# A one-core perceiver block with state-space scan and routed experts: groups of 2,4,4,4,2 batches instead of four of 4, an earlier first expert wave, and the key bias moved into the exponential

## The chip, the cores and the metric

One Trainium2 chip, one of its cores. The metric is the device time of one execution in microseconds, the median of several runs. All arithmetic is 32-bit floating point.

## What is computed

Sixteen batches of 64 tokens, width 512, go through three blocks with residual connections; each batch has a context of 512 rows.

```python
x = x + xattn(layernorm(x), ctx, ctx)        # softmax(q k^T / 8) v with biases bq, bk, bv
x = x + mamba(layernorm(x))                  # 1024 channels, 16 states per channel:
    xc    = silu(conv4(x @ Wx))
    delta = softplus(x @ Wdt + b)
    h     = exp(delta * A) * h + delta * B_t * xc       # for each token in turn
    y     = sum_s h_s * C_ts + D * xc ;   out = y @ Wout
x = x + ffn(layernorm(x))                    # 16 experts, 4 for each token, chosen by a
                                             # grouped top-k on sigmoid(x @ Wg) + e_bias
```

The reference reshapes queries and keys so that each batch falls into two independent attention units (even and odd rows of tokens and context): 8 heads x 32 queries = 256 query rows against 256 keys. There are 32 units. The key bias gives a term q·bk that is the same for all keys of a query row.

## The kernel before

**Groups.** The batches are worked off in groups (`GBS`, L58): four groups of 4 batches, that is 256 tokens, 2 token tiles of 128 and 8 attention units each. A group goes through attention and the projections (B and C, delta, x with its convolution). Its 16 states are then scanned while the *next* group is in attention. One state (`scan_step`, L1308) is four VectorE passes over 128 x 2048: input product L1317, scan L1320, product with C (L1324 or L1327), and, where it is done on VectorE, the addition to y (L1331). ScalarE makes the decay of each state before (`scan_decay`, L1072, eight exponentials).

**Sums on TensorE.** For groups 0 to 2 (`SUMMED`, L105) the addition to y is done by TensorE instead: `start_sum` (L655) and `sum_state` (L661) multiply by the identity into four PSUM banks, 8 instructions of 512 columns for a state, and `copy_sum` (L1055) takes the sum out. For group 3 VectorE adds (L1331).

**An attention unit.** `scores` (L669): 16 matmul instructions of 256 columns (L677), and for each half of the query rows one more with 8 rows of contraction that adds the key-bias term to every key (L678, 4 instructions for a unit). VectorE takes the negated maximum (`neg_max`, L1256), ScalarE exponentiates with that as bias (L969) and normalises, TensorE transposes the probabilities (L687) and multiplies by the context (L699, 16 instructions). Before the units of a group stands `attn_prep` (L606): queries L613, key-bias term L619, queries times key weights L643; behind them the value projection L730, then `projections` (L744, L759), and at the end of the loop `out_proj` (L767) for the group before.

**Scan beside attention.** In each stage four states run in the preparation (`LEAD`), eight beside the units (`unit_states`, L110), two before and two behind the layer norm of the next group (`TAIL`, `PRE`). The end of a stage on VectorE is `scan_inputs` (L1289, its second pass is L1295), after which the next group's scan can start.

**Experts.** Tokens are routed (`ffn_norm`, `ffn_logits`, `route`, `positions`, `slots`) and scattered by GpSimd into DRAM rows grouped by expert (`dispatch`, L1605), which must have been cleared to zero first (L1598 to L1603, 40 transfers of up to 1 MB from a zero tile, gated on score units 8 to 15). `WAVES` (L68) splits the groups in two waves: groups 0 to 2, 6 tiles, 39 blocks of 128 rows; group 3, 2 tiles, 23 blocks. A block is: transposes L788, gate and up L798 (8 instructions of 512 columns), hidden on ScalarE and VectorE (L1138, L1468, L1469), transposes L807, down L819 (4 instructions), and 2 MB of DMA, three quarters of it expert weights. The loop `experts` (L823) runs the same order on PE, ACT and DVE; wave 0 begins only when group 2 has been routed, which happens after the attention of group 3, and SyncE's queue waits there for the block table (`expert_of`, L417) and for all tokens dispatched (L447). Beside wave 0, `scan_parts` (L116) lays out the 14 states of group 3 that are left, spread over steps -1 to 28. `OUT_STEP` (29 = 39 - `REST`) is the step behind which the output projection and the routing of group 3 stand in every engine's order. Two PSUM banks each serve for the transposed blocks (0, 1) and for the block outputs (4, 5). Wave 1 follows; GpSimd gathers each token's four expert rows (`collect`, L1614), VectorE combines them (L1477), SyncE stores the tile.

The order on every engine is written out by hand in these loops; PE, ACT, DVE, POOL and the SP queue each follow their own in-order program and wait on semaphores.

Of the kernel before, what the change touches and what calls it, by code (L numbers as in the profile page):

```python
# [27 lines left out]
P = 128  # L28
# [29 lines left out]
GBS = (4, 4, 4, 4)  # L58
# [9 lines left out]
WAVES = ((0, 1, 2), (3,))  # L68
# [7 lines left out]
CLEARS = [(w, r, min(r + CLEAR_ROWS, ROWS[w])) for w in range(len(WAVES)) for r in range(0, ROWS[w], CLEAR_ROWS)]  # L76
CLEAR_UNITS = range(8, 16)
# [3 lines left out]
REST = 10  # L81
OUT_STEP = BLOCKS[0] - REST
# [19 lines left out]
LEAD, TAIL, PRE = 4, 2, 2  # L102
LN_AFTER = 3
SCAN_PARTS = 4
SUMMED = range(NGR - 1)  # L105
# [4 lines left out]
def unit_states(g, k):  # L110

    n = NS - LEAD - TAIL - 2
    return list(range(LEAD + k * n // NUS[g + 1], LEAD + (k + 1) * n // NUS[g + 1]))


def scan_parts(q):  # L116

    n0 = 2 * SCAN_PARTS
    return [(n // SCAN_PARTS, n % SCAN_PARTS) for n in range(n0, NS * SCAN_PARTS)
            if (n - n0) * (BLOCKS[0] + 1 - REST) // (NS * SCAN_PARTS - n0) - 1 == q]  # L120


def a_jobs():

    out = [("norm", 0)] * NTS[0]
    for g in range(NGR):
# [3 lines left out]
        out += [("query_ctx", g)] * (DC * DC // 2)  # L130
# [21 lines left out]
def perceiver_block(nc, x, ctx_t, ctx_n, wq_t, wk_w, wv_t, xp_t, dt_t, bc_t, ow_t, gate_t,  # L152
                    eg_t, eu_t, ed_t, params, bc_dram, out):
    with ExitStack() as es:
# [52 lines left out]
        rsum = sb("row_sum", 2 * QB)  # L207
        ones8 = sb("ones", 1)
# [32 lines left out]
        wb_ = [sb(f"expert_w_{s}", 2 * DC * I + IC * D)[:, :] for s in range(NW)]  # L241
        w_gu = [v[:, 0:2 * DC * I].rearrange("p (g c i) -> p g c i", g=2, c=DC) for v in wb_]
        w_dn = [v[:, 2 * DC * I:].rearrange("p (c d) -> p c d", c=IC) for v in wb_]
        xbT = [sb(f"block_x_t_{s}", D)[:, :].rearrange("p (c t) -> p c t", c=DC) for s in range(2)]
        route_ = sb("route_scratch", 4 * QB * KEYS)
# [4 lines left out]
        xb = [sb(f"block_x_{s}", D)[:, :] for s in range(NX)]  # L250
        yb = [sb(f"block_y_{s}", D)[:, :] for s in range(NX)]
        pick_ = sb("route_pick", TOPK * 6 * E)
        sb("unused_2", 2 * SW - NX * 2 * D - TOPK * 6 * E)
        acc_last = sb("y_acc", SW)
        acc_s = [(dA[(NS * (g + 1) - 1) % NDEC] if g in SUMMED else acc_last)[:, 0:NBK * GTS[g]] for g in range(NGR)]
        acc = [v.rearrange("p (k t) -> p k t", k=NBK) for v in acc_s]

        def route_buffers(c):

            n = NT * E * E  # L260
            if c < NGR - 2:
                return hs_[:, 0:n], hs_[:, n:2 * n], hs_[:, 2 * n:2 * n + 2 * TOPK * NT * E]
            return route_[:, 0:n], route_[:, n:2 * n], pick_[:, :]
# [53 lines left out]
        sb8_rdy = sem("qbk_ready")  # L317
        q_full = sem("ctx_queries_full")
# [19 lines left out]
        cleared = sem("dispatch_rows_cleared")  # L338
# [23 lines left out]
        D_LAST = sum(NTS) + sum(NTS[:NGR - 1])  # L362
# [14 lines left out]
        def _(sp):  # L377
# [104 lines left out]
            for g in range(NGR - 1):  # L482
# [9 lines left out]
                for s in range(NS - TAIL, NS):  # L492
                    load_bc(g * NS + s)
                load_proj(g + 1)
                store_bc(g + 1)
                load_bc((g + 1) * NS)
                load_bc((g + 1) * NS + 1)
            sp.wait_ge(ys_rdy, NGR)
            load_bc((NGR - 1) * NS + 2)
            for w in range(len(WAVES)):  # L500
                n = BLOCKS[w]
                if w == 0:
                    for j in range(NW):
                        load_gate_up(w, j)
                        load_down(w, j)
                    for j in range(NX):
                        load_block_x(w, j)
                    load_bc((NGR - 1) * NS + 3)
                for j in range(-2, n + 1):
# [15 lines left out]
                    if w == 0:  # L525
                        for state, part in scan_parts(j - 1):
                            if part == SCAN_PARTS - 1 and state + 2 < NS:
                                load_bc((NGR - 1) * NS + state + 2)
# [9 lines left out]
        def _(pe):  # L538
# [67 lines left out]
            def attn_prep(g):  # L606
# [15 lines left out]
                if g > 0:  # L622
                    start_sum(g - 1)
# [8 lines left out]
                for c in range(DC):  # L632
                    for mp in range(2):
# [13 lines left out]
                        if mp == 0:  # L647
                            mm.then_inc(q_full, 1)
# [1032 lines left out]
```

## Time and profile before

| | us |
|---|---|
| median of 3 runs (1382.69 to 1383.88) | 1383.72 |
| the profiled execution | 1382.23 |
| its span, first to last instruction | 1380.4 |
| TensorE busy with matmuls | 1190.3 (86%) |
| VectorE busy | 871.5 (63%) |
| ScalarE busy | 629.5 (46%) |
| DMA moved | 266 MB, mean 193 GB/s |

The profiled execution lies 1.5 us under the median, and 1.8 us of it lie outside the span. Busy shares are averages over stages with different limits. The busy time of matmuls is modelled and overlaps, so the pace of a loop is better read from the distance between two starts of the same step than from busy time. A row of the chain of waits gives start, length and what ran; the next start minus the last is the pace.

### The profile page before, as it was taken

The numbers are of one execution on the slowest core, as the hardware profiler recorded it, in microseconds if no ns is written. First come the engines' busy times: TensorE is split into PE (matmuls) and PEld (weight loads), VectorE is DVE, ScalarE is ACT, GpSimd is POOL, SyncE is SP. The second block draws the span as 40 slices with busy tenths as digits, with TensorE's granted clock in tenths as the row PEclk, the third lists the DMA queues.
The fourth block names the chain that finished last, engine by engine and source line by source line (L and its number), as shares of the span: only waits on it lengthen the run. The fifth ranks groups of instructions, "written<-read, shape, count | busy, mean of one in ns | idle before, by whom it ended". The sixth has DMA issues, their size and how long they took to land.

```text
span 1380.4 us, 13494 instructions
## 1 busy us (share of the span) xinstructions
PE 1190.3 (86%) x4404; PEld 738.6 (54%) x4404; DVE 871.5 (63%) x882; ACT 629.5 (46%) x1394; POOL 132.5 (10%) x113
## 2 busy tenths in 40 slices
PE   5996869888897899999799999835999999999993
PEld 4774745555574566666456666532444444544451
DVE  1211279655858779785897987685999993323312
ACT  4442566334356745536665563642545441222231
POOL 0010002211000006000003300011000000223002
PEclk9998989889999999999999999957999998999997
DMA  7346104999510034440013424018899993999993
GB/s 271 101 136 256 42 16 141 407 406 328 181 61 8 16 91 154 129 143 12 16 36 99 148 61 141 5 49 295 318 374 359 367 373 115 370 364 407 411 387 122
DMA packets 114038, 266.22 MB, mean 193 GB/s; under 512 B 10161, under 2 KB 43057, under 8 KB 113969
## 3 DMA queue, kind: packets, MB, share of 16 engines
q1 hardware_dynamic: 98096, 207.16, 43.3%
q0 software_dynamic: 15872, 58.20, 10.8%
q8 instruction: 36, 0.59, 0.2%
q14 instruction: 34, 0.27, 0.1%
HBM read 197.03 MB, written 68.29 MB: 192 GB/s over the span
## 4 chain that ended last, share of the span: by engine, by line
PE 60%; DVE 22%; ACT 7%; DMA 7%; issue 3%; POOL 1%; SPq 0%; POOLq 0%; DVEq 0%; ACTq 0%
PE bank L665 10%; PE bank L677 9%; PE bank L798 8%; PE bank L699 7%; PE bank L759 7%; DVE state L1320 6%; PE bank L819 4%; DVE state L1317 3%; PE bank L678 3%; DMA ctx<-in_ctx_t 3%; DVE state L1327 2%; DVE y_acc L1331 2%; PE bank L613 2%; PE bank L730 2%; ACT decay L1082 2%
## 5 line engine op out<-in xcount | busy, mean ns | idle before, releaser
L1320 DVE TENSOR_TENSOR_SCAN state<-decay,state 128x2048 f32<-128x2048 f32 x64 | 282.9, 4420 | 22.0 <-ACT decay L1082 21.1
L798 PE MATMUL bank<-expert_w,block_x_t 128*128 128x512 f32 x496 | 226.3, 599 | 3.0 <-ACT block_x_t L1134 2.6
L665 PE MATMUL bank<-decay,params 128*128 128x512 f32 x384 | 178.7, 610 | 5.1 <-DVE decay L1324 5.1
L1082 ACT ACTIVATE decay<-delta_even,params 128x256 f32<-128x256 f32 x256 | 107.2, 499 | 115.2 <-PE bank L665 106.7
L1611 POOL DMA_INDIRECT dispatched<-ffn_x,slot x32 | 71.0, 2218 | 796.3 <-DVE slot L1413 787.7
L677 PE MATMUL bank<-ctx,queries_ctx 128*128 128x256 f32 x512 | 133.2, 406 | 13.8 <-DMA ctx<-in_ctx_t 12.6
L798 PEld LDWEIGHTS bank<-expert_w,block_x_t 128*128 128x128 f32 x496 | 91.2, 194 | 94.6 <-issue 91.5
L1082 ACT ACTIVATE decay<-delta_odd,params 128x256 f32<-128x256 f32 x256 | 106.3, 499 | 56.8 <-PE bank L665 47.1
L699 PE MATMUL bank<-probs,ctx 128*128 128x256 f32 x512 | 121.8, 393 | 11.2 <-ACT probs L991 6.8
L699 PEld LDWEIGHTS bank<-probs,ctx 128*128 128x128 f32 x512 | 99.8, 197 | 37.6 <-issue 16.7
L819 PE MATMUL bank<-expert_w,hidden_t 128*128 128x512 f32 x248 | 117.0, 594 | 2.9 <-ACT hidden_t L1148 2.9
L677 PEld LDWEIGHTS bank<-ctx,queries_ctx 128*128 128x128 f32 x512 | 97.5, 200 | 40.6 <-issue 15.7
L665 PEld LDWEIGHTS bank<-decay,params 128*128 128x128 f32 x384 | 71.2, 193 | 88.0 <-issue 81.3
L759 PE MATMUL bank<-normed_t,queries_ctx 128*128 128x256 f32 x512 | 113.6, 382 | 4.3 <-DMA queries_ctx<-in_dt_t 3.2
L1468 DVE SCALAR_TENSOR_TENSOR hidden<-hidden,bank 128x256 f32<-128x256 f32 x62 | 26.1, 421 | 143.0 <-ACT hidden L1138 136.0
L1324 DVE TENSOR_TENSOR decay<-state,bc_bcast 128x2048 f32<-128x2048 f32 x48 | 109.5, 2282 | 0.8
L759 PEld LDWEIGHTS bank<-normed_t,queries_ctx 128*128 128x128 f32 x512 | 97.4, 191 | 22.6 <-issue 4.5
L1317 DVE TENSOR_TENSOR state<-u_even,bc_bcast 128x2048 f32<-128x2048 f32 x32 | 73.4, 2293 | 36.6 <-DMA bc_bcast<-bc_scratch 35.7
L1138 ACT ACTIVATE hidden<-bank 128x256 f32<-128x256 f32 x62 | 23.6, 381 | 145.7 <-PE bank L798 136.7
L819 PEld LDWEIGHTS bank<-expert_w,hidden_t 128*128 128x128 f32 x248 | 46.8, 190 | 61.1 <-issue 57.4
L1317 DVE TENSOR_TENSOR state<-u_odd,bc_bcast 128x2048 f32<-128x2048 f32 x32 | 73.3, 2290 | 2.0 <-DMA bc_bcast<-bc_scratch 1.3
L1144 ACT ACTIVATE block_y<-bank 128x512 f32<-128x512 f32 x62 | 37.0, 597 | 80.7 <-PE bank L819 76.7
(193 smaller groups left out, 1391.8 us busy)
## 6 DMA issues: line engine op xcount, KB each, us to landing
dispatched<-ffn_x POOLq DMA_DIRECT2D x38, 1024.0 KB, 22.8
expert_w<-in_eg_t SPq DMA_DIRECT2D x62, 512.0 KB
expert_w<-in_eu_t SPq DMA_DIRECT2D x62, 512.0 KB
expert_w<-in_ed_t SPq DMA_DIRECT2D x62, 512.0 KB
ctx<-in_ctx_t SPq DMA_DIRECT2D x32, 512.0 KB, 6.9
ctx<-in_ctx_n SPq DMA_DIRECT2D x32, 512.0 KB, 4.2
bc_bcast<-bc_scratch SPq DMA_DIRECT2D x64, 256.0 KB, 5.9
block_x<-dispatched SPq DMA_DIRECT2D x62, 256.0 KB
```

The costliest lines, as they stand in the source:

```text
L665: mm = pe.matmul(y_bank[c][:, :], ident, dA[(g * NS + j) % NDEC][:, c * 512:(c + 1) * 512], start=False, stop=(j == NS - 1))
L677: pe.matmul(o, QT[g][:, k, c, qb * P:(qb + 1) * P], ctxT[n % 2][:, c, :], start=(c == 0), stop=False)
L678: mm = pe.matmul(o, sb8[g][:, k, qb * 4:(qb + 1) * 4, :], ones8[0:H, :].to_broadcast([H, KEYS]), start=False, stop=True)
L699: mm = pe.matmul(b[:, cc * Q:(cc + 1) * Q], ctxN[n % 2][:, j, c * P:(c + 1) * P], probT[n % 2][:, j, :], start=(j == 0), stop=(j == KC - 1))
L759: mm = pe.matmul(b[:, kk * gt:(kk + 1) * gt], w[:, c, (k + kk) * P:(k + kk + 1) * P], xT[g][:, c, :], start=(c == 0), stop=(c == DC - 1))
L798: mm = pe.matmul(o, xbT[q % 2][:, c, :], w_gu[q % NW][:, :, c, :], start=(c == 0), stop=(c == DC - 1))
L819: mm = pe.matmul(bank[4 + q % 2][:, :], hidT[q % 2][:, c, :], w_dn[q % NW][:, c, :], start=(c == 0), stop=(c == IC - 1))
L1082: ins = act.activation(dA[n % NDEC][:, k * gt:(k + 1) * gt], dlt[g][:, k, :], ACT.Exp, scale=par[:, c:c + 1])
L1317: step(dve.tensor_tensor(h3, u[g], bs, ALU.mult))
L1320: dve.tensor_tensor_scan(h, dA[n % NDEC][:, 0:sw], h, 0.0, ALU.mult, ALU.add).then_inc(scan_rd, 1)
L1324: dve.tensor_tensor(hc, h3, cs, ALU.mult).then_inc(step_done, 1)
L1611: pool.indirect_dma_start(xd[WAVE_OF[c]], bass.IndirectOffsetOnAxis(slot[:, i:i + 1].bitcast(U32), 0), fx[:, t, :], None).then_inc(dispatc ...
```

## The change

- Groups of 2, 4, 4, 4, 2 batches: 5 groups, the first and last with 128 tokens, one tile, 4 units and states 1024 wide. `GBS = (2, 4, 4, 4, 2)`.
- Waves (0,1,2) and (3,4): 5 tiles and 35 blocks, then 3 tiles and 27 blocks. Group 2 is routed during the attention of group 4, so nothing of wave 0's routing stands behind the last projections.
- Sums on TensorE for groups 1 and 2, and for the first 11 states of group 3; the rest (group 0, the last 5 states of group 3, group 4) is added on VectorE.
- The last 5 states of group 3 and all 16 of group 4 run beside the first steps of wave 0, laid out by weight (a scan counts double, a group by its batches). Output projection and routing of group 3 come at step 10, 11 and 13, those of group 4 at 28, 29 and 31 (`REST` 7).
- The key-bias matmuls L678 go; `row_bias` makes the term as one column for each unit half in `attn_prep`, ScalarE copies it, and `neg_max` takes it off and puts it on again in two small VectorE passes.
- One PSUM bank for block transposes (0) and one for block outputs (1), since banks 4 and 5 serve the output projections in wave 0.
- The clearing of wave 0's rows (24 transfers) moves to units 1 to 11, that of wave 1 (16 transfers) to units 14 to 21, and takes its zeros from cleared rows in DRAM.
- Weights of blocks 0 and 1 and the first three x blocks are fetched before the last group's y is started; the weights of block 2 behind it.

```diff
-GBS = (4, 4, 4, 4)
+GBS = (2, 4, 4, 4, 2)
-WAVES = ((0, 1, 2), (3,))
+WAVES = ((0, 1, 2), (3, 4))
-CLEAR_UNITS = range(8, 16)
+CLEAR_UNITS = [range(1, UNIT0[2]), range(UNIT0[2] + 2, UNIT0[3] + 2)]
-REST = 10
-OUT_STEP = BLOCKS[0] - REST
+REST = 7
-LEAD, TAIL, PRE = 4, 2, 2
+LEAD = 4
+UNIT_STATES = [NS - 8] * (NGR - 2) + [4]
+TAIL = [2] * (NGR - 2) + [1]
+PRE = [2] * (NGR - 2) + [2]
-SUMMED = range(NGR - 1)
+SUM_END = {g: NS for g in range(1, NGR - 2)}
+SUM_END[NGR - 2] = LATE
+def scan_work():
+    n0, n1 = (NGR - 2) * NS + LATE, NGR * NS
+    todo = [(n, p, GBS[n // NS] * (2 if p == 1 else 1)) for n in range(n0, n1) for p in range(SCAN_PARTS)]
+    total = sum(v for _, _, v in todo)
+    out = {j: [] for j in range(-1, BLOCKS[0])}
+    gone = 0
+    for n, p, v in todo:
+        out[gone * (BLOCKS[0] + 1 - REST) // total - 1].append((n, p))
+        gone += v
+    return out
+OUT_STEP = {NGR - 2: step_of((NGR - 1) * NS - 1, SCAN_PARTS - 1) + 1, NGR - 1: BLOCKS[0] - REST}
...
+            def row_bias(g):
                 pe.wait_ge(sb8_rdy, g + 1)
+                b = job_a()
+                for k in range(NUS[g]):
+                    for qb in range(QB):
+                        mm = pe.matmul(b[:, k * QB + qb:k * QB + qb + 1], sb8[g][:, k, qb * 4:(qb + 1) * 4, :], ones8[0:H, :],
+                                       start=True, stop=True)
+                mm.then_inc(a_full, 1)
...
-                        pe.matmul(o, QT[g][:, k, c, qb * P:(qb + 1) * P], ctxT[n % 2][:, c, :], start=(c == 0), stop=False)
-                    mm = pe.matmul(o, sb8[g][:, k, qb * 4:(qb + 1) * 4, :], ones8[0:H, :].to_broadcast([H, KEYS]),
-                                   start=False, stop=True)
+                        mm = pe.matmul(o, QT[g][:, k, c, qb * P:(qb + 1) * P], ctxT[n % 2][:, c, :],
+                                       start=(c == 0), stop=(c == DC - 1))
...
+                step(dve.tensor_reduce(nm, bank[n % 2][:, :].rearrange("p (b k) -> p b k", b=QB), AX_X, ALU.max, negate=True))
+                if k == 0:
+                    dve.wait_ge(rowb_rdy, g + 1)
+                step(dve.tensor_tensor(nm, nm, add, ALU.subtract))
+                dve.tensor_tensor(nm, nm, add, ALU.add).then_inc(nm_rdy, 1)
...
-                if q >= 2:
-                    pe.wait_ge(xt_rdy, q - 1)
+                if q >= 1:
+                    pe.wait_ge(xt_rdy, q)
...
+                    for c, out_step in OUT_STEP.items():
+                        if w == 0 and j == out_step:
+                            out_proj(c)
+                        if w == 0 and j == out_step + 1:
+                            ffn_logits(c)
+                        if w == 0 and j == out_step + 3:
+                            positions(c)
```

## Rows read from the trace of the kernel before

**Rows 1.** The chain of waits, whole span: start us, us, what (ends of stages).
```profile
174.94 2.30 DVE queries_ctx L1295
...
422.57 2.30 DVE queries_ctx L1295
...
656.66 2.30 DVE queries_ctx L1295
...
886.94 2.30 DVE queries_ctx L1295
...
950.22 4.20 PE bank L798 x8
```
**Rows 2.** The same chain: units of the first stage and of the third.
```profile
79.57 3.65 PE bank L699 x16
88.56 3.65 PE bank L699 x16
...
542.91 3.63 PE bank L665 x8
546.54 3.45 PE bank L699 x16
555.34 3.63 PE bank L665 x8
```
**Rows 3.** Table by stretch: busy PE, PEld, DVE, ACT, POOL, PEclk, DMA share, GB/s.
```profile
245.00:350.00 105.00, 85.93 (x302) 57.30 (x301) 57.37 (x31) 45.22 (x115) 18.35 (x25) 0.89 0.98 381
...
736.00:820.00 84.00, 81.68 (x325) 56.27 (x325) 68.37 (x46) 46.05 (x117) 25.28 (x8) 1.00 0.33 110
...
880.00:950.00 70.00, 27.97 (x97) 19.49 (x96) 50.84 (x96) 26.66 (x55) 13.31 (x8) 0.62 0.32 113
950.00:1138.00 188.00, 180.76 (x546) 90.39 (x544) 180.15 (x116) 91.54 (x218) 0.00 (x0) 1.00 0.96 348
```
**Rows 4.** The chain of waits in the expert waves.
```profile
1062.90 4.43 DVE state L1320
...
1075.91 4.44 DVE state L1320
...
1217.89 3.70 PE bank L798 x8
...
1346.94 3.44 PE bank L798 x8
```
**Rows 5.** Groups of instructions, the key-bias matmul: xcount, busy us, mean ns, idle before.
```profile
L678 PE MATMUL bank<-ones,normed 8*128 8x256 f32 x128 | 45.2, 432 | 0.0
```
**Rows 6.** Timeline, PE and DVE: the first score, and small operations used as prices.
```profile
36.86 1.97 PE L677 MATMUL bank<-ctx,queries_ctx 128*128 128x256 f32 x8 [1.19 <-issue]
...
688.87 1.93 PE L581 MATMUL bank<-gate_weights,probs 128*128 128x16 f32 x16 [0.87 <-ACTq L898]
...
696.10 0.69 DVE L1349 TENSOR_TENSOR state<-state,params 128x512 f32<-128x512 f32 x1
```
**Rows 7.** DMA issues, us 245 to 350: xcount, KB each, us to landing.
```profile
ctx<-in_ctx_t SPq DMA_DIRECT2D x6, 512.0 KB, 18.2
```
**Rows 8.** Timeline behind step 29: output projection and routing of group 3.
```profile
1138.71 15.67 PE L777 MATMUL bank<-out_w,y_acc 128*128 128x512 f32 x32 [1.74 <-issue]
...
1154.42 0.69 DVE L1266 TENSOR_TENSOR x_tokens<-x_tokens,bank 128x512 f32<-128x512 f32 x1 [6.18 <-PE bank L777]
...
1157.41 1.00 DVE L1251 TENSOR_SCALAR ffn_x<-x_tokens,mean_var,rstd 128x512 f32<-128x512 f32 x2
...
1165.61 0.18 DVE L1361 TENSOR_SCALAR route_score<-route_logits 128x32 f32<-128x32 f32 x1 [5.28 <-ACTq L904]
...
1173.98 0.19 DVE L1390 TENSOR_TENSOR route_score<-route_score,route_group 128x32 f32<-128x32 f32 x1
```
**Rows 9.** Timeline of the tail: the combination of the last two tiles.
```profile
1368.79 3.11 DVE L1477 SCALAR_TENSOR_TENSOR x_tokens<-y_top,top_weight,x_tokens 128x512 f32<-128x512 f32 x4 [17.08 <-DMA y_top<-expert_out,expert_out_slot]
...
1374.87 3.12 DVE L1477 SCALAR_TENSOR_TENSOR x_tokens<-y_top,top_weight,x_tokens 128x512 f32<-128x512 f32 x4 [2.97 <-DMA y_top<-expert_out,expert_out_slot]
```

More of the change, by code:

```diff
@@ L110, in unit_states, with summed, sum_count, step_of @@
 def unit_states(g, k):
-    n = NS - LEAD - TAIL - 2
+    n = UNIT_STATES[g]
     return list(range(LEAD + k * n // NUS[g + 1], LEAD + (k + 1) * n // NUS[g + 1]))
[L116 to L120, printed above, removed]
+def summed(n):
+    return n // NS in SUM_END and n % NS < SUM_END[n // NS]
+def sum_count(n):
+    return sum(summed(k) for k in range(n + 1))
+def scan_work():
[8 more added lines that the diff above has]
+    return out
+SCAN_WORK = scan_work()
+def step_of(n, part):
+    return next(j for j, v in SCAN_WORK.items() if (n, part) in v)
+OUT_STEP = {NGR - 2: step_of((NGR - 1) * NS - 1, SCAN_PARTS - 1) + 1, NGR - 1: BLOCKS[0] - REST}
 def a_jobs():
@@ L207, in perceiver_block @@
         rsum = sb("row_sum", 2 * QB)
+        rowb_ = sb("row_bias", 2 * NU * QB)
+        rowb = [rowb_[:, g % 2 * NU * QB:(g % 2 + 1) * NU * QB] for g in range(NGR)]
         ones8 = sb("ones", 1)
@@ L337, in perceiver_block @@
         zero_rdy = sem("zero_rows_ready")
-        cleared = sem("dispatch_rows_cleared")
+        cleared = [sem(f"dispatch_rows_cleared_{w}") for w in range(len(WAVES))]
         cst_rdy = sem("index_constants_ready")
@@ L525, in _ @@
                     if w == 0:
-                        for state, part in scan_parts(j - 1):
-                            if part == SCAN_PARTS - 1 and state + 2 < NS:
-                                load_bc((NGR - 1) * NS + state + 2)
+                        for k, part in SCAN_WORK.get(j - 1, []):
+                            if part == SCAN_PARTS - 1 and k + 2 < NGR * NS:
+                                load_bc(k + 2)
                     elif j % 2 == 0 and (j - 6) // 2 in range(len(WTILES[0])):
@@ L740, in attention @@
                 if g > 0:
-                    for s in range(NS - TAIL - PRE, NS - PRE):
+                    for s in range(TAIL0[g - 1], PRE0[g - 1]):
                         sum_state(g - 1, s)
@@ L1109, in projections @@
             def projections(g):
-                late = list(range(NS - TAIL + 1, NS)) if g > 0 else []
+                late = list(range(TAIL0[g - 1] + 3, min(NS, LATE + 2 if g == NGR - 1 else NS))) if g > 0 else []
                 norm_std(NTS[g])
@@ L1116, in projections @@
                     proj_dt(g, k)
-                    if late:
+                    if late and k in (0, NBK - 2):
                         scan_decay(g - 1, late.pop(0))
@@ L1536, in _ @@
                             out_slots(0)
-                late = list(range(NS - TAIL - 2, NS))
-                for s in range(TAIL):
-                    scan_step(g, late.pop(0))
+                for s in range(TAIL0[g], PRE0[g]):
+                    scan_step(g, s)
                 add_tiles(g + 1)
@@ L1545, in _ @@
                     norm_apply(TILE0[g + 2], NTS[g + 2], NT, mv1_, rstd1, TILE0[g + 2])
-                for s in range(PRE):
-                    scan_step(g, late.pop(0))
+                for s in range(PRE0[g], PRE0[g] + PRE[g]):
+                    scan_step(g, s)
                 for k in range(0, NBK, 2):
@@ L1622, in collect @@
                         .then_inc(yg_in[n % 2], 16)
-            for c in range(NGR):
+            pool.wait_ge(zero_rdy, 1)
+            clear(0)
+            dispatch(0)
+            clear(1)
+            for c in range(1, NGR):
                 dispatch(c)
```

237 lines of the change are left out of this document (124 added, 113 removed).

## The prediction

> **What bounds the kernel now.** I read the chain of waits first, to cut the span into stages at VectorE's `scan_inputs` (L1295): the stages end at 174.9, 422.6, 656.7 and 886.9 us, so they last 174.9, 247.6, 234.1 and 230.3 us, and then 63.3 us pass until the first gate matmul of the experts [rows 1]. Inside a stage the chain shows TensorE: a unit of the first stage takes 8.99 us, one of a later stage 12.43 us, of which 3.44 us more are the sum of one state [rows 2]. The table by stretch confirms it, TensorE 81.7 of 84 us busy, VectorE only 68.4 [rows 3]. Two stretches stand out. Between 880 and 950 TensorE is busy 28 of 70 us at a mean clock of 0.62: group 2 is routed, dispatched and its blocks fetched, with nothing else to do. Between 245 and 350 the DMA engines are 0.98 busy and TensorE loses 19 us: the clears. In wave 0 the chain goes over to VectorE: two blocks and one state of group 3 come every 13.01 us, against a block every 5.87 us in wave 1 (22 distances from 1217.89 to 1346.94), where TensorE and nearly the DMA set the pace [rows 4].
>
> **The change, stage by stage.** The sum is made against the profiled execution (span 1380.4, time 1382.23); the median of the runs is 1.5 us higher.
>
> *Key bias.* An L678 instruction has 256 columns like those of L699, 16 of which take 3.45 us in the chain, so 0.216 us each (0.217 with the seams); 4 in a unit are 0.87 us and 128 are 27.8 us (the 45.2 us of its group are overlapping busy time) [rows 2, 5]. The new `row_bias` has 128 instructions of one column. The nearest row has 16 columns and the same 128 weights to load: 16 in 1.93 us, 0.12 us each, so 15 us [rows 6]. It stands where ScalarE's copies and VectorE's states set the pace, so I put 0.5 us on the path in each stage; the ends are 0 and 3 us for each. The Trainium skill (TensorE: Matmul & The Clock Gate, Wait — 56ns, not 53.3ns?) has the gap between matmuls as the number of columns in cycles, by which `row_bias` would be nearly free; the row of L581 speaks against it, and the sum with the rule would be some 2 us shorter. The two small VectorE passes are about 0.2 us each. They lie in a unit where VectorE has 10.5 of 11.6 us to do, and in the first stage where it idles.
>
> *Narrow states.* No row has 1024 columns. A pass of 512 takes 0.69 us and one of 2048 2.30 us [rows 1, 6], 1.04 ns a column, so 1024 take 1.22 us (between 1.15, half of 2.30, and 1.3); a scan 4.43/2 + 0.03 = 2.25 us [rows 4]. A narrow state, added on VectorE, is 3 x 1.22 + 2.25 + gaps = 6.0 us; a wide one 11.35 us.
>
> *Stage 0* (2 batches, 4 units). The first score stood at 36.9 us [rows 6]; with half the width before it, but fixed costs kept, 28.5. 8 units at 8.99 were 72 us; 4 at 8.99 - 0.87 = 8.13 are 32.5. The other 66 us (ends of the unit pipeline, value, norm, projections, convolution) become 48, half wide where columns count, bound in part by ScalarE's fixed costs, and with the statistics of the other tiles now in the last unit, 3 us of them. 109 us, **-66**.
>
> *Stage 1* (8 units beside group 0). I start from stage 3, which had no contention, 230.3 us. Units at 8.13 instead of 12.43 take off 34; eight sums outside the units and `start_sum`, 9 x 3.6 us, take off 31, some of it through decays that are half as wide: 165. Then the clears: 24 of 1 MB in 11 units of stages 0 and 1 instead of 38 in 8. Per unit there are 2.2 MB of clears, 1.05 of context, 0.2 of B and C, 3.4 MB in 8.1 us, 420 GB/s: over the 381 GB/s of the saturated stretch [rows 3], at which a unit takes 9.0 us. I charge 8 us, all of it here (0 to 32, below): 173 us, **-75**.
>
> *Stages 2 and 3* are as before less 8 x 0.87 us and plus 0.5 us of `row_bias`; stage 2 has the 16 clears from DRAM to DRAM beside it, for which no row exists: 3 us (0 to 10). 231 and 224 us, **-3 and -6**.
>
> *Stage 4* is new (4 units, 11 wide states of group 3). From the 224 us of stage 3: 4 units of 11.56 less, 46; the projections' 128 matmul instructions at 0.12 instead of 0.217 us, 12; value 4; one tail state less before the norm, partly hidden, 4. `block_table` and `out_slots` now stand in unit 1 on a nearly full VectorE, 5 more. The 4 MB of projection weights that are fetched a fifth time land behind the norm and wait for nothing new; if they do, up to 5 us. **+162**. Stages together: 899 us for 886.9, +12.
>
> *The gap* between the last `scan_inputs` and the first gate matmul was 63.3 us [rows 1]. Tokens are dispatched and weights fetched a stage earlier; what is left is the rest of `scan_inputs`, y's start (8 narrow copies) and a copy of the block: 6 us, **-57**. What it hid (group 2's output projection) is in stage 4.
>
> *Wave 0* lasted from 950.2 to 1217.9, 267.7 us [rows 1, 4]. After: 5 wide states, 56.8 us, 16 narrow ones, 96 us, and 29 hidden pairs of 0.86 us, 25 us, are 178 us in 29 slots, 6.1 a block; TensorE needs 5.87. New are group 3's output projection and routing in the middle of it. VectorE idled some 14 us while the 15.67 us of L777 ran, then took 4 us to the end of the norm and 8.6 us for `route`, and slots and waits are 4 more [rows 8]. That was harmless behind the last state; now VectorE bounds on both sides, so 31 us count. With 4.5 us before the first hidden and 3 of friction: 216.5 us. From there to wave 1: 7.8 us for one tile of L777, then 5 gate and 7 down matmul groups with their transposes, 37 us, logits and positions 4: 49 us of TensorE. The data chain beside it is a little longer: 11 us from the projection's end to the logits as in [rows 8], 7 `route`, 8 to the positions (they wait for step 31), 2 slots, 6 dispatch, 6 landing, 3 for the block: 52 us. Together 268 us, **0**, though there are 4 blocks fewer.
>
> *Wave 1* has 27 blocks for 23: 4 x 5.87 = **+23.5**. A single bank for transposes and one for outputs I put at nothing: ScalarE, busy 92 of 188 us even in wave 0 [rows 3], copies them within the step, before the next use a step later; if decays hold it up, a copy's 0.6 us for each such block. *The tail* has a third tile, and two tiles are 6.1 us apart: **+6** [rows 9].
>
> Sum: -66 - 75 - 3 - 6 + 162 - 57 + 0 + 23.5 + 6 = -15.5 us. Span 1365, execution 1367, median 1368 us.
>
> **Rivals.**
>
> *Clears stop the first stages* (slower). While the clears had the queues, a context load took 18.2 us to land [rows 7]. Loads are issued two units ahead of their scores, so at that latency a unit can't be shorter than about (18.2 + 4)/2 = 11 us, 3 over 8.1, and 11 units lose 32 us instead of my 8: 1392 us. It decides if clears queue up, that is if more than about 8.1 x 0.4 = 3.2 MB fall in a unit; the sum above has 3.4, just over. For it: the saturated stretch. Against it: there 5 MB of clears fell in a unit of 12.4 us, and a backlog of 23 built up that can't build up with two or three in a unit. 0.12. The Trainium skill (DMA: Bandwidth & Descriptors, Queues, rings and completion order) has each engine take its queues in turn, by which a context load would wait for few clear packets, and this rival would fall; the 18.2 us of [rows 7] don't bear out an even share.
>
> *Waves don't mesh* (about no change). The routing of group 4 now has 7 steps instead of 10 to reach the dispatched rows, SyncE's queue stops at step 31 for the block table with the store of block 30 and the down weights of block 33 behind it, and wave 0's states slip past their slots. If the middle stall is 40 and the seam 8 us more, +17: 1385 us. 0.13.
>
> *The early stages give more* (faster). No contention (-8), narrow stages' fixed costs smaller (-8), and part of the stall around step 10 filled, because TensorE can run a block ahead (-8): 1344 us. For it: ScalarE is only 46% busy. 0.23.
>
> *It doesn't do what it says*: wave 0 is held at its start by the dispatch or by weights and the gap stays half, +25, 1393. Group 2's slots come in unit 1 of stage 4, over 80 us before; 0.03.
>
> **The numbers.** The forecast, 1368 (its own reach 1355 to 1380), has 0.49. A measurement of this kernel can tell about 0.2%, 2.8 us, from no change. Faster: the forecast, the fast rival and a little of the second, 0.76. Same: 0.08. Slower: the first and fourth rival and the rest, 0.16. The range goes from the fast rival with some room, 1338, to the contention rival, 1392.
>
> **What would show it.** The stages' ends at about 109, 282, 513, 737 and 899 us; units of 8.1 to 9 us in the first two stages and 11.6 after; the first L798 near 905; in wave 0 VectorE idle for some 14 us before L1266 at step 10; wave 1 from about 1173. If the ends of stages 0 and 1 come 20 us late with waits for `ctx`, the first rival holds; if the first L798 lies above 930, the gap did not close.

## The result, and the profile after

The changed kernel takes 1436.34 us (median of 4 runs, 1433.52 to 1441.55) against 1383.2 for the kernel before (4 runs): a ratio of 1.0397, 95% interval 1.0365 to 1.0429. Forecast were 1368 us and a range of 1338 to 1392. It is 53 us slower where 15 us less were expected. The profiled execution took 1441.55 us, its span is 1439.8.

The first view is the timeline of VectorE in the changed kernel, the second pass of `scan_inputs` (now L1361), whose five starts end the stages; the summary gives the shortest, median and longest duration in ns and the first and last start of each group.

```profile
L1361 DVE SCALAR_TENSOR_TENSOR queries_ctx<-queries_ctx,u_even x3: 1224/1227/2293, 114.7 to 955.7; 128x1024 f32<-128x1024 f32 x2, 128x2048 f32<-128x2048 f32 x1
L1361 DVE SCALAR_TENSOR_TENSOR queries_ctx<-queries_ctx,u_odd x2: 2291/2292/2292, 303.7 to 783.7; 128x2048 f32<-128x2048 f32 x2
```

The third of the `u_even` starts is at 555.57. With the first gate matmuls of wave 0 (962.66) and wave 1 (1249.92), from the chain of waits, the span falls into the pieces of the forecast. The last column is experiment e4, told below.

| piece | forecast | after | e4, clears moved |
|---|---|---|---|
| stage 0 | 109 | 114.7 | 107.6 |
| stage 1 | 173 | 189.0 | 168.8 |
| stage 2 | 231 | 251.9 | 225.5 |
| stage 3 | 224 | 228.1 | 227.2 |
| stage 4 | 162 | 172.0 | 170.6 |
| gap to wave 0 | 6 | 7.0 | 7.0 |
| wave 0 | 268 | 287.3 | 284.1 |
| wave 1 and tail | 192 | 189.9 | 189.2 |
| span | 1365 | 1439.8 | 1379.9 |

Three pieces stand out, stages 1 and 2 and wave 0. The chain of waits of the changed kernel shows what stands there (start us, us, what). It answers to [rows 2] and [rows 4]:

```profile
168.64 14.98 DMA ctx<-in_ctx_t
183.67 5.52 PE bank L732 x16
194.38 10.11 DMA ctx<-in_ctx_t
204.53 5.33 PE bank L732 x16
215.04 9.55 DMA ctx<-in_ctx_t
...
405.64 3.46 PE bank L732 x16
412.53 3.47 PE bank L753 x16
416.01 0.37 SPq L428
416.44 0.46 SPq L452
416.94 34.24 DMA ctx<-in_ctx_t
451.23 6.55 PE bank L732 x16
...
1092.98 13.41 DMA bc_bcast<-bc_scratch
...
1144.48 11.07 DMA bc_bcast<-bc_scratch
...
1176.31 8.81 DMA bc_bcast<-bc_scratch
```

In the units of [rows 2] the chain was TensorE from end to end. Now three context loads of 9.6 to 15 us stand in stage 1, one of 34 us in stage 2, and loads of B and C in wave 0. Those of stage 1 are not new: the chain of the kernel before has two there too, in the stretch with its clears, which [rows 2] does not cover:

```profile
253.13 17.65 DMA ctx<-in_ctx_t
...
288.70 17.69 DMA ctx<-in_ctx_t
```

New are the load in stage 2, which had no clears before, and the B and C loads of wave 0, of which the kernel before has none in its chain. The list of waits of the changed kernel says the same in sums (us in total, times, longest):

```profile
DVE state L1383 <- DMA bc_bcast<-bc_scratch: 66.1, 16, 23.9
...
PE bank L732 <- DMA ctx<-in_ctx_t: 44.1, 6, 24.0
...
ACT row_bias L1006 <- PE bank L704: 25.2, 5, 6.7
```

The timeline of stage 2, DMA issues and scores, shows who is ahead of the late load:

```profile
406.16 1.54 SPq L420 DMA_DIRECT2D ctx<-in_ctx_t  x1
406.77 2.02 POOL L1677 DMA_INDIRECT dispatched<-ffn_x,slot  x1 [0.30 <-issue]
408.78 3.96 POOL L1668 DMA_DIRECT2D dispatched<-dispatched  x8
...
416.94 0.46 SPq L420 DMA_DIRECT2D ctx<-in_ctx_t  x1
...
420.17 0.96 POOL L1668 DMA_DIRECT2D dispatched<-dispatched  x2 [7.43 <-PE bank L732]
...
427.21 15.43 SPq L452 DMA_DIRECT2D bc_bcast<-bc_scratch  x1
442.68 4.01 SPq L420 DMA_DIRECT2D ctx<-in_ctx_t  x1
449.82 2.29 DVE L1383 TENSOR_TENSOR state<-u_odd,bc_bcast 128x2048 f32<-128x2048 f32 x1 [23.86 <-DMA bc_bcast<-bc_scratch]
...
451.23 6.55 PE L732 MATMUL bank<-ctx,queries_ctx 128*128 128x256 f32 x16 [24.03 <-DMA ctx<-in_ctx_t]
```

Read it from the second row down. GpSimd finishes the dispatch of group 0 (L1677), for whose slots it had waited since its last clear in stage 1, and then issues **eight** clears of 1 MB within 4 us. Their gates are 14 to 17 score units, two for each, but in its in-order program they stand behind the dispatch, and by then all four gates had passed. The context load issued at 416.94 lands 34 us later, the next B/C issue takes 15.43 us on SyncE's queue, and TensorE and VectorE both stand still for 24 us. An average over the stage hides this. The table by stretch, for stage 2 after and then in e4 (columns as in [rows 3], with instruction counts), has the same work in both and even the lower DMA share where the wait is. A stretch of 10 us inside the wait, the third fence, shows what the average hides: the DMA engines are 0.98 busy, at 334 GB/s, and nothing else runs.

```profile
303.70:555.60 251.90, 203.37 (x820) 141.49 (x819) 184.24 (x168) 128.31 (x286) 18.38 (x18) 0.89 0.41 130
```
```profile
276.30:501.90 225.60, 200.12 (x816) 139.11 (x815) 184.24 (x168) 128.49 (x286) 17.34 (x16) 0.94 0.46 135
```
```profile
430.00:440.00 10.00, 0.00 (x0) 0.00 (x0) 0.00 (x0) 0.00 (x0) 0.00 (x0) 0.50 0.98 334
```

With the two clears of 420.17, ten of 1 MB were issued in 12 us. At 334 GB/s they and the loads beside them take some 31 us or more (an estimate from these rows), about the 34 us that the context load took.

### The profile page after: what moved, and what is told of

Its sections match the earlier page's. It is cut to its first block, busy times and chain, and to the rows that moved or that the text cites. A ratio compares the mean times of both kernels' runs of the same rounds, so it can differ in the third digit from the quotient of the medians.

```text
span 1439.8 us, 14536 instructions
## 1 busy us (share of the span) xinstructions
PE 1186.8 (82%) x4662; PEld 774.0 (54%) x4662; DVE 913.8 (63%) x1084; ACT 675.7 (47%) x1602; POOL 122.7 (9%) x113
## 3 DMA queue, kind: packets, MB, share of 16 engines
q0 software_dynamic: 12096, 58.20, 10.8%
## 4 chain that ended last, share of the span: by engine, by line
PE 53%; DVE 21%; DMA 11%; ACT 10%; issue 3%; SPq 2%; POOL 1%; POOLq 0%; DVEq 0%; ACTq 0%
PE bank L720 8%; PE bank L852 8%; PE bank L813 7%; DVE state L1386 6%; PE bank L732 6%; DMA ctx<-in_ctx_t 6%; PE bank L753 5%; PE bank L871 4%; ACT decay L1145 3%; DVE state L1383 3%; DMA bc_bcast<-bc_scratch 2%; PE bank L784 2%; PE bank L655 2%; PE bank L704 2%; PE bank L685 2%
## 5 line engine op out<-in xcount | busy, mean ns | idle before, releaser
L1386 DVE TENSOR_TENSOR_SCAN state<-decay,state 128x2048 f32<-128x2048 f32 (+1 forms) x80 | 285.5, 3568 | 39.6 <-ACT decay L1145 38.4
L852 PE MATMUL bank<-expert_w,block_x_t 128*128 128x512 f32 x496 | 234.3, 617 | 1.0 <-ACT block_x_t L1199 1.0
L732 PE MATMUL bank<-ctx,queries_ctx 128*128 128x256 f32 x512 | 130.6, 415 | 48.1 <-DMA ctx<-in_ctx_t 44.1
L720 PE MATMUL bank<-decay,params 128*128 128x512 f32 x344 | 162.5, 618 | 0.0
L1145 ACT ACTIVATE decay<-delta_even,params 128x128 f32<-128x128 f32 (+1 forms) x384 | 132.4, 427 | 40.2 <-PE bank L720 33.7
L732 PEld LDWEIGHTS bank<-ctx,queries_ctx 128*128 128x128 f32 x512 | 105.4, 210 | 68.3 <-DMA ctx<-in_ctx_t 45.9
L1677 POOL DMA_INDIRECT dispatched<-ffn_x,slot x32 | 65.6, 2050 | 728.1 <-DVE slot L1481 719.9
L813 PE MATMUL bank<-normed_t,queries_ctx 128*128 128x256 f32 (+1 forms) x640 | 120.2, 351 | 8.8 <-DMA queries_ctx<-in_dt_t 5.4
L813 PEld LDWEIGHTS bank<-normed_t,queries_ctx 128*128 128x128 f32 x640 | 107.3, 202 | 24.5 <-DMA queries_ctx<-in_dt_t 6.5
L1383 DVE TENSOR_TENSOR state<-u_even,bc_bcast 128x1024 f32<-128x1024 f32 (+1 forms) x48 | 75.9, 1581 | 40.7 <-DMA bc_bcast<-bc_scratch 39.6
L1390 DVE TENSOR_TENSOR decay<-state,bc_bcast 128x2048 f32<-128x2048 f32 x43 | 98.1, 2282 | 0.8
```

The costliest lines, as they stand in the source:

```text
L720: mm = pe.matmul(y_bank[c][:, :], ident, dA[(g * NS + j) % NDEC][:, c * 512:(c + 1) * 512], start=False, stop=(j == SUM_END[g] - 1))
L732: mm = pe.matmul(o, QT[g][:, k, c, qb * P:(qb + 1) * P], ctxT[n % 2][:, c, :], start=(c == 0), stop=(c == DC - 1))
L813: mm = pe.matmul(b[:, kk * gt:(kk + 1) * gt], w[:, c, (k + kk) * P:(k + kk + 1) * P], xT[g][:, c, :], start=(c == 0), stop=(c == DC - 1))
L852: mm = pe.matmul(o, xbT[q % 2][:, c, :], w_gu[q % NW][:, :, c, :], start=(c == 0), stop=(c == DC - 1))
L1145: ins = act.activation(dA[n % NDEC][:, k * gt:(k + 1) * gt], dlt[g][:, k, :], ACT.Exp, scale=par[:, c:c + 1])
L1383: step(dve.tensor_tensor(h3, u[g], bs, ALU.mult))
```

## The experiments

Each ratio is to the kernel before on the same chip, with its 95% interval. Lengths of stages come from the starts of `scan_inputs` in each trace, as above.

**e1: the key bias alone.** The kernel before, with `row_bias`, its copy and the two small passes instead of L678, that is, from L678 to the last line on `neg_max` in the diff above.

> The kernel before with the key bias in the exponential and nothing else of the change. Theory A (the size is what the units show): a unit of the changed kernel's second stage is 10.8 us long where one of before is 12.4, so the four key-bias matmuls cost 1.65 us and not 0.87; 32 units give 53 us back, row_bias makes ScalarE wait 5.3 us in each of 4 preparations, 21 us: net 25 to 32 us faster, 1352 to 1358. Rival B (my forecast's sizes, 0.87 us a unit and 0.5 us a stage): 26 us faster in stages, 2 to 7 us for each stage of 8 units, with units of 11.6 us. Rival C: VectorE's two small passes and row_bias eat it up, within 5 us of before. The length of a unit in the third stage tells A (10.2 to 10.8) from B (11.6); the preparation's length tells the cost of row_bias.

1377.37 us, ratio 0.9951 (0.9932 to 0.997). The unit of stage 2 went from 12.43 to 10.78 us: an L678 costs 0.41 us, not 0.217. The 432 ns "mean of one" in [rows 5], which I had put aside as overlap, was nearly right. But the preparation, from the end of a stage to the first score, grew from 58.5 us (422.57 to 481.02) to 68.3 (425.02 to 493.32). Its timeline:

```profile
470.12 6.63 PE L665 MATMUL bank<-ones,normed 8*128 8x1 f32 x32 [3.48 <-ACT queries_ctx L955]
...
476.79 0.18 ACT L963 ACTIVATE row_bias<-bank 128x16 f32<-128x16 f32 x1 [6.33 <-PE bank L665]
...
482.40 3.30 ACT L1100 ACTIVATE decay<-delta_odd,params 128x256 f32<-128x256 f32 x8 [5.43 <-PE bank L679]
```

ScalarE's copy of 16 columns lies between the copies of queries and the next decay, and ScalarE stands still for 6.33 us until the 32 instructions of one column are through. Most of what the units of a stage gain, 8 x 1.65 = 13.2 us, is given back there. Theory A had the unit right and the total wrong: 6 us faster, not 25 to 32, nearest to rival C.

**e2: B/C loads of wave 0 on GpSimd's queue.**

```diff
-sp.dma_start(bcs[k % 2] ...)      # in SyncE's program, beside wave 0
+pool.dma_start(bcs[k % 2] ...)    # in GpSimd's, behind the dispatch
```

> The changed kernel, with the loads of B and C beside wave 0 issued from GpSimd's queue, which idles there, instead of behind the expert weights on SyncE's queue. Theory A (a queue's order): in wave 0 VectorE waits 13.4, 11.1 and 8.8 us for bc_bcast because their issue stands behind the wait of SyncE's queue for a block; the waits go, and wave 0 (287 us from its first gate matmul to wave 1's) gets 20 to 30 us shorter, 1406 to 1416. Rival B (DMA traffic, or VectorE's own work, sets wave 0): the waits stay or move into the passes, less than 8 us.

1445.01 us, ratio 1.0451, and 288.7 us between the first gate matmuls of the waves, for 287.3: nothing gained. The chain shows each load still as a piece of its own:

```profile
1121.34 8.02 DMA bc_bcast<-bc_scratch
...
1136.61 8.52 DMA bc_bcast<-bc_scratch
...
1152.31 7.79 DMA bc_bcast<-bc_scratch
...
1167.35 7.86 DMA bc_bcast<-bc_scratch
```

SyncE's queue was not the cause. As rival B said, the waits stay. A load starts when the state two before it is done and lands 8 us later; a narrow state takes 6.

**e3: wave 1's clears late; e4: all clears in the preparations.** The clears are gated on scan states of the preparation instead of score units: in e3 wave 1's in the preparation of stage 3; in e4 also wave 0's, half in that of stage 1 from the zero tile, half in that of stage 2 from cleared rows in DRAM.

```diff
-pool.wait_ge(s_full, CLEAR_UNITS[w][...])
+pool.wait_ge(step_done, g * NS + s)      # s = 1, 2, 3; dl_rdy for the first quarter
```

> The changed kernel, with the 16 DRAM-to-DRAM clears of wave 1's rows moved from the units of stage 2 to the preparation of stage 3's successor stage, where the DMA engines idle. Theory A (clears hold up context loads): the wait of 34 us in stage 2 goes, the stage falls from 252 to 222 to 230 us, and nothing comes back elsewhere: 20 to 28 us faster, 1408 to 1416. Rival B (the wait had another cause, SyncE's queue or the small B and C loads): a long wait for ctx stays in stage 2, less than 8 us. Rival C: the wait moves to the new place, B and C loads late in the preparation, 5 to 15 us net.

> The changed kernel, with all 40 clears in preparations: 12 of wave 0 from the zero tile in stage 1, 12 from DRAM in stage 2, 16 of wave 1 in stage 3. Theory A: stages 0 and 1 lose their waits for ctx too (12.5 and 8.9 us, and 15, 10 and 10 us in the chain), so beside the 20 to 28 us of the run before 20 to 40 us more come back: 1375 to 1395. Rival B (the early waits are first loads at the kernel's start, not clears): stages 0 and 1 stay at 115 and 189 us, 1405 to 1416.

e3: 1409.57 us, ratio 1.0182 (1.016 to 1.0205), stage 2 225.1 us long instead of 251.9. e4: 1379.82 us, ratio 0.997 (0.9951 to 0.9989), with the stages of the table above. The wait of the scores for `ctx_t`, 44.1 us, is no longer among the waits of e4, and this is left of the other:

```profile
DVE state L1383 <- DMA bc_bcast<-bc_scratch: 20.3, 10, 6.2
```

So the place of the clears costs 56.5 us: 27 in stages 0 and 1, 26 in stage 2, the rest behind. The bytes written are the same; twelve of wave 0's transfers now read DRAM instead of the zero tile. In the preparations of stages 2 and 3 they cost nothing that shows (225.5 us against 225.1 without them in e3, 227.2 against 228.1). For stage 1 no run of the changed kernel has a preparation without clears.

**e5: four B/C buffers for the narrow states.** On top of e4; a narrow state fills half of a buffer, so each is split in two.

```diff
-bs, cs = (bcs[n % 2][:, w * gt:(w + 1) * gt] ...
+buf = bcs[n % 2] if n < NARROW else bc4[(n - NARROW) % 4]
+bs, cs = (buf[:, w * gt:(w + 1) * gt] ...
...
+sp.wait_ge(step_done, max(k - 3, NARROW - 1 + i // 2) if i < 4 else k - 3)    # before: k - 1
```

> Clears in the preparations as in the run before, and for the 16 narrow states the two B/C buffers are split into four, so that a load is issued when the state four before it is done instead of two before. Theory A (the latency of a B/C load, about 8 us, is longer than a narrow state and a half, and with two buffers bounds wave 0): from the first gate matmul of wave 0 to that of wave 1 becomes 284 - 12 = 272 us, and the time 1379.8 - 12 = 1368 us; no B/C load stands in the chain of waits. Rival (VectorE's own work and the slots bound the wave; the loads are what the chain shows last by accident, VectorE sat idle for them only 16.5 us): -3 us or less, 1377 to 1380.

1368.36 us, ratio 0.9894 (0.9859 to 0.9928), 11.5 us less than e4. Wave 0 is 268.4 us long (908.69 to 1177.07), and in its chain the only DMA piece is the first block of wave 1. Beside wave 0, VectorE was idle for B/C 16.5 us in e4, about the 15.7 us by which the wave is shorter (268.4 for 284.1).

**e6, e7, e8: no key-bias term.** The term is the same for all keys of a query row and cancels in the softmax. These kernels leave it out altogether: no `key_bias`, no `row_bias`, no L678 or small passes. e6 is e4 without it, e7 the kernel before without it, e8 e5 without it.

```diff
-key_bias(g) ... row_bias(g)
-step(dve.tensor_tensor(nm, nm, add, ALU.subtract))
-dve.tensor_tensor(nm, nm, add, ALU.add).then_inc(nm_rdy, 1)
```

> Clears in the preparations, and the key-bias term is left out altogether (it is the same for all keys of a query row and cancels in the softmax): no key_bias, no row_bias, no two small VectorE passes. Theory A (row_bias, its wait on PE and ScalarE's wait for it lengthen each preparation by 8 to 10 us, since ScalarE's copies and decays pace it): each of the stages 1 to 4 becomes 8 us shorter, stage 0 some 6, in all 35 us: 1345 us. Rival (the preparation is longer for another reason, the order of states and decays): row_bias is worth its 0.5 us a stage that I had charged, 1376 us.

> The kernel before with the key-bias term left out altogether. Against the kernel before with the bias in the exponential (1377.4 us), theory A: 8 to 10 us less in each of stages 1 to 3 and 6 in stage 0, 1345 us. Rival: 1375 us. If this kernel is as fast as or faster than the changed one with quiet clears and no bias, the groups of 2, 4, 4, 4, 2 bring nothing of their own.

> Both together: clears in the preparations, no key-bias term, four B/C buffers for the narrow states. If the two parts are independent, their gains add: 1379.8 - 35 - 12 = 1333 us by the A theories, 1374 us by the rivals.

e6: 1348.03 us (ratio 0.9738, 0.9703 to 0.9773), 32 less than e4. e7: 1327.92 (0.9586, 0.9546 to 0.9626), 49 less than e1; its four stages are shorter than e1's by 13.8, 10.0, 11.3 and 10.0 us, and the preparation is 55.0 us (401.23 to 456.25) instead of 68.3. e8: 1338.77 (0.967, 0.9634 to 0.9706), 41 us less than e4 where e5 and e6 alone gave 11.5 and 32. In the kernel before with `row_bias`, the whole bias (`key_bias`, `row_bias` and the two small passes) costs what theory A said and more; in the changed one it costs that in stages 0 and 2 and less in the others (e4 to e6: 8.8, 3.6, 9.3, 3.9 and 3.0 us), which I did not follow up.

**e9, e12: the kernel before with quiet clears.** e12 moves only the clears, as in e4 (14 in the preparation of stage 1, the rest of wave 0's in that of stage 2, wave 1's in that of stage 3); e9 also leaves the key-bias term out.

> The kernel before without the key-bias term and with its clears moved out of the units: 14 transfers from the zero tile in the preparation of stage 1, 13 to 14 from cleared rows in DRAM in that of stage 2, those of wave 1 in that of stage 3. Theory A (clears beside units cost what they keep context loads waiting): its second stage, 243.5 us without bias, becomes as long as its third, about 220, and the time 1328 - 22 = 1306 us. Rival (its units had room for the clears, and the new places cost as much in stages 2 and 3): 1320 to 1335 us.

> The kernel before, key bias by matmul as it was, with only its clears moved to the preparations as in the run above. Theory A: its second stage becomes 232 us instead of 247.6, and the time 1383 - 16 = 1367 us. Then the changed kernel with quiet clears (1379.8) is slower than the kernel before with quiet clears by some 13 us, which is what the rest of the change costs. Rival: units of 12.4 us had room for the clears, 1380 us.

e12: 1347.42 us, ratio 0.974 (0.9699 to 0.9781). The kernel before paid 36 us for its clears, twice what I read from it and what theory A said: 29 in stage 1 (218.7 us instead of 247.6), 6 in stage 0. With quiet clears in both and the bias in each as it was, the changed kernel is 32 us slower (e4 against e12). e9: **1294.11 us, ratio 0.936** (0.9323 to 0.9397), the fastest of all, faster than both kernels, and 12 us under theory A. The page of e9 and then of e8, the changed kernel with the same two mends and four B/C buffers:

```profile
span 1287.1 us, 13136 instructions
PE 1119.3 (87%) x4244; PEld 718.0 (56%) x4244; DVE 871.1 (68%) x882; ACT 619.0 (48%) x1362; POOL 125.2 (10%) x113
```
```profile
span 1338.4 us, 14067 instructions
PE 1134.1 (85%) x4494; PEld 733.8 (55%) x4494; DVE 903.3 (67%) x1020; ACT 660.7 (49%) x1557; POOL 118.7 (9%) x113
```

The rest of the change brings 250 matmul instructions and 15 us of TensorE more, and 32 us of VectorE, for the same computation. That is more than the smaller groups: VectorE also adds the five states that TensorE no longer sums (43 of them at 8 instructions for 48), and no run separates the groups from the sums, the waves and the banks.

**e10, e11: packets and transfer size.** Two tries at why clears hurt. e10 cuts wave 1's clears in single rows, e11 makes all clears a quarter as large.

```diff
-xd[w][first:end].rearrange("(p r) d -> p r d", p=P)    # e10
+xd[w][first:end].rearrange("(r p) d -> p r d", p=P)
-CLEAR_ROWS = 512                                       # e11
+CLEAR_ROWS = 128
```

> The changed kernel, with wave 1's clears cut in elements of one row of 2 KB instead of four adjoining rows for a partition; same bytes, same places in units 14 to 21. Theory A (the large packets of the DRAM-to-DRAM transfers hold each DMA engine so long that context and B/C loads wait): with 2 KB packets the third stage falls from 252 to about 235 us and the time from 1436 to 1420 us. Rival (what counts is the bytes, 16 MB read and 16 MB written beside 8 units): 1433 to 1441 us; if small packets are themselves dearer, above.

> The changed kernel with all clears in transfers of 128 rows instead of 512, four times as many, spread evenly over the same units. Theory A (what hurts is a queue of two or three 1 MB transfers started together, ahead of a context load): the first two stages lose 10 to 20 us of their 304, the third as much of its 252, 1410 us. Rival (the bytes in a unit decide, or a fourfold number of issues on GpSimd costs): 1433 to 1445 us.

e10: 1436.91 us (ratio 1.0381, 1.0337 to 1.0425). The packets did become smaller; the queue that carries the clears, us 368 to 500, first after, then e10 (queue: packets, MB, share of 16 engines):

```profile
q0 software_dynamic: 768, 15.73, 33.2%
```
```profile
q0 software_dynamic: 4128, 15.73, 35.7%
```

Stage 2 took 247.7 us, and the time is the same. e11: 1445.68 (1.0439, 1.039 to 1.0487), no better. Both theories A fall: neither packets five times smaller nor transfers four times smaller let the loads through.

**e13, e14: pace.** By now the cluster of eight at 408.78 had been seen. Both kernels are the changed one with other gates for wave 1's clears: e13 two for each of the units 17 to 24, e14 one for each of the units 17 to 21, then group 1's dispatch, then eleven over units 22 to 28.

```diff
-range(UNIT0[2] + 2, UNIT0[3] + 2)
+range(UNIT0[2] + 5, UNIT0[3] + 5)      # e13
```

> The changed kernel with the gates of wave 1's clears moved by three units (17 to 24 instead of 14 to 21), so that GpSimd meets them after the dispatch of group 0 and issues two at each unit instead of ten within 12 us. Theory A (a backlog of 8 to 10 MB, read and written, is what context and B/C loads wait behind; two a unit, with 1.25 MB of loads, just fit in 10.8 us at the 318 GB/s of the saturated stretch): no wait for ctx over 5 us, stage 2 about 230 and stage 3 about 231 us instead of 252 and 228, time 1436 - 19 = 1417 us. Rival (each MB beside units costs its 1.7 us wherever it lies): stages 2 and 3 together stay at 480 us, 1433 to 1440 us.

> The changed kernel with wave 1's clears spread thinner: one at each of the units 17 to 21, the dispatch of group 1, and the other eleven over units 22 to 28. Theory A: nothing is saturated any more, stages 2 and 3 as with clears in the preparations (225 and 228 us), 1436 - 26 = 1410 us. Rival: 480 us for both stages, 1433 to 1440 us.

e13: 1426.72 us (1.0318, 1.0271 to 1.0365), between theory A's 1417 and the rival's 1433; stage 2 231.1 us, as theory A said, stage 3 235.5, 4 more than it said: there four clears were issued within 4.4 us. e14: 1438.04 (1.0397, 1.0335 to 1.0459), no gain, a time that the rival had. Its timeline says why:

```profile
421.44 0.52 POOL L1674 DMA_DIRECT2D dispatched<-dispatched  x1 [10.58 <-PE bank L732]
...
432.21 0.49 POOL L1674 DMA_DIRECT2D dispatched<-dispatched  x1 [10.25 <-PE bank L732]
...
442.99 0.49 POOL L1674 DMA_DIRECT2D dispatched<-dispatched  x1 [10.29 <-PE bank L732]
...
651.71 3.96 POOL L1674 DMA_DIRECT2D dispatched<-dispatched  x8
...
665.34 18.99 SPq L452 DMA_DIRECT2D bc_bcast<-bc_scratch  x1
684.38 3.80 SPq L420 DMA_DIRECT2D ctx<-in_ctx_t  x1
693.54 5.30 PE L732 MATMUL bank<-ctx,queries_ctx 128*128 128x256 f32 x16 [28.20 <-DMA ctx<-in_ctx_t]
```

I made the mistake of the change again: the dispatch of group 1 reached its slots only in the middle of stage 3, and behind it eight clears came out at once and two more within the next 4 us. With one clear to a unit, four in all, stage 2 is 225.0 us long, the same as with none beside it (225.1 in e3). With twelve clears, ten of them in 8 us, stage 3 is 257.8 us long for 227.2. At the 1.7 us for each MB of e13's rival that would be 7 and 20 us; measured are 0 and 31, so the rival had the total and not the places. Stage 2 of e14 had fewer bytes too, so the cleanest comparison is e13 with the changed kernel: the same 16 MB, all beside units of stages 2 and 3, cost 14 us two at a time (466.6 us for both stages) and 28 us with the cluster (480.0), against 452.2 in e3. Issued evenly they cost half; in the preparations nothing.

## Why the prediction was wrong

**Clears: the step that failed.** "I charge 8 us" for wave 0's and "3 us (0 to 10)" for wave 1's. They cost 27 and 26, and 56.5 with what came behind: 45 of the 68 us between forecast and result. Two errors lie in it. I averaged megabytes over units (3.4 MB a unit), as if the gates in the diff were the times of issue. For wave 1's the order on GpSimd decides: dispatch of group 0 first, then whatever gates have passed meanwhile. What is queued behind a waiting instruction the prediction counted on SyncE ("stops at step 31") and not on GpSimd, whose order (`clear(0)`, `dispatch(0)`, `clear(1)`) stood in the code. Wave 0's clears have no dispatch ahead of them; they too came closer together than an average says (seven between 162.5 and 172.7 us), but no run changed their pace alone, so how the 27 us arise inside stages 0 and 1 stays open. And I sized the contention of the kernel before by stage 1 less stage 3, 17 us; it was 36 (e12). Without clears its stage 1 takes 218.7 us, 12 less than the 230.3 of stage 3 that I started from. Set side by side, clears cost the kernel before 35 us in its first two stages and the changed one 27; what the change added is the 26 of stage 2.

**The first rival** (clears stop the first stages, 1392 us) had the place of the 27 us of stages 0 and 1, where it put 32, and what waits (`ctx`), but not the 26 of stage 2. Its signs are there in part: stage 1 ends at 303.7 for 282, stage 0 only 6 us late. Its threshold of 3.2 MB a unit was not tested in its stages; in stage 2 what counts is how many clears come out together. Its sentence on the Trainium skill (DMA: Bandwidth & Descriptors, Queues, rings and completion order) stands as put: if the engines took their queues in turn in equal parts, a load of 0.5 MB would take some 3 us at half of the 334 GB/s (an estimate), not 34. The section has the turn end with a whole packet; five times smaller packets (e10) did not change the time, so no run here shows that as the cause.

**The gain that was none.** The forecast's differences are taken from a kernel whose stages 0 and 1 hold its own clears, so part of the forecast -15.5 us was clears taken away: the 36 that they cost before less the 11 that I charged after, 25 us. Without them the same sum says 9.5 us slower; measured are 32 (e4 against e12). e9 and e8, both with quiet clears and without the bias, and e8 with four B/C buffers, give the price of the rest of the change, the groups 2, 4, 4, 4, 2 with the waves, sums and banks that go with them: stages 872.9 for 795.8 us (+77), gap 6.8 for 63.2 (-56), gate matmuls first to last 419.1 for 393.3 (+26), tail 39.6 for 34.8 (+5): 51 us of span, ratio 0.967 against 0.936. The gap closed exactly as forecast (7.0 us for 6), and this was not enough to pay for the fifth stage.

**Key bias.** The unit gained 1.65 us, not 0.87 (10.8 us where I had 11.6); `row_bias` cost about 10 us in a stage of four batches, not 0.5 (ends 0 and 3, both too low). Two things were missed. The 32 instructions took 5.6 to 7.0 us, 0.17 to 0.22 each for 0.12. The granted clock was 0.63 to 0.50 there, behind 3.5 us in which TensorE waited for ScalarE, while my row of L581 ran at 1.00; 0.174 x 0.63 and 0.218 x 0.50 both give 0.11 us at that clock (an estimate), so the price was right and the clock was not. And I missed who waits: "where ScalarE's copies and VectorE's states set the pace" was the reason to count it, not to leave it out. The two errors pull against each other but do not cancel: e1 gains 6 us where the steps sum to 26 (27.8 less 4 x 0.5). By the sizes measured in stage 2 it would be 14 (32 x 1.65 less 4 x 9.8). e1's stage 1, the one with the clears, is 5.9 us longer than before (253.5 for 247.6); why was not tested.

**Wave 0** 287.3 for 268. Narrow passes (1.225 us) and scans (2.29) are as forecast, and the first eleven slots too (71.5 us). What failed is what follows: two buffers and 8 us to landing bound a 6 us state. With four buffers it is 268.4 (e5); that this meets the 268 is in part luck, since the seam below is longer than I had it. The stall around the output projection in the middle, for which I had 14 us, is 12.5 us in e4, in two waits of VectorE for L831 (6.3 and 6.2). The latency of the B/C load was in no step, a term put at nothing without a reason, though [rows 7] was read for context loads. The rival of waves that don't mesh looked in the right piece for the wrong cause (SyncE's order, e2). The seam, from group 4's output projection to wave 1, is 57.8 us for 52; this I did not test.

**Stage 4** 172 for 162, of which the clears are 1. Its projection weights are on the chain for 8 us, where I had "up to 5" for them if they were late; the bias takes 3 us there (e6); the rest is open. **Stages 0, 1, 2, 3** without the clears (107.6, 168.8, 225.5, 227.2) lie within 6 us of the forecast, with both bias errors and the base of stage 1, 12 us too long, in them, so this is in part luck, and wave 1 with the tail within 3.

## What to carry to other kernels

Gates in a program are not times of issue: follow each queue in order, and ask which of its instructions are held back together and come out together when the one ahead of them is released. Put bulk transfers where no load with a deadline is outstanding; one megabyte to a unit was free here (four of them), two to a unit cost 6 to 8 us in a stage, eight at once stopped TensorE and VectorE for 24 us or more. When a short operation on one engine is put between two others of a busy second engine, price the wait of the second, and when tiles are halved, check whether the latency of their loads still fits the number of buffers.

## What the runs showed that was not expected

- A matmul instruction with 8 rows of contraction and 256 columns costs 0.41 us (1.65 us for four, 12.43 to 10.78 us a unit), about twice one with 128 rows (0.217 us), both at a granted clock of 1.00.
- A matmul instruction of one column (8 rows of contraction) with new weights costs hardly less than one of 16 columns (128 rows), some 0.11 for 0.12 us at full clock, an estimate: it took 0.17 us at a granted clock of 0.63 (32 in 5.58 us, after), 0.22 us at 0.50 (32 in 6.96 us, after), and the one of 16 columns 0.12 us at 1.00. A price taken from a row at one clock does not hold for a place with another.
- Two DMA issues on SyncE's queue, most of which take 0.4 to 1.5 us, take 15 and 19 us while a cluster of clears on GpSimd's queue is outstanding (427.21 after, 665.34 in e14). What holds the issue itself is open.
- Copies from DRAM to DRAM in a preparation are all but free: 12 MB in stage 2 left it at 225.5 us for 225.1 (e4, e3), 16 MB in stage 3 at 227.2 for 228.1 (e4, after). In the kernel before, 12 MB in stage 3 went with 234.6 us for 230.3 (e12, before) and 220.9 for 219.1 (e9, e7).
